# Cross attention on one core: probabilities transposed in 32x32 blocks on DVE, context in sixteen 32x32 tiles of TensorE

## What is computed

```python
q = x @ Wq + 2 * (x @ Aq @ Bq)        # x (8, 256, 1024), 32 heads of 32
k = c @ Wk + 2 * (c @ Ak @ Bk)        # c (8, 256, 1024), 8 key heads of 32
v = c @ Wv + 2 * (c @ Av @ Bv)        # each key head serves 4 query heads
attn = softmax(q @ k.T / sqrt(32))    # per head, 256 x 256
context = attn @ v
out = x + context @ Wo + 2 * (context @ Ao @ Bo)
```

## Time and profile before

| | before |
|---|---|
| median of 3 runs | 756.59 us (755.97 to 759.47) |
| span of the profiled execution | 753.1 us; the page gives no other time for it |
| PE, DVE, ACT, POOL busy | 98%, 62%, 51%, 46% |
| DMA | 117.01 MB, mean 155 GB/s |

### The profile page before, as it was taken

How to read it: one execution, slowest core, us unless ns; L and a number is a source line. 1 busy time by engine, 2 the same in 40 slices (tenths; PEclk the granted TensorE clock), 3 DMA queues, 4 the chain that set the end, 5 groups by cost and what they waited for, 6 DMA issues and landing times.

```text
span 753.1 us, 17856 instructions
## 1 busy us (share of the span) xinstructions
PE 737.6 (98%) x5776; PEld 645.2 (86%) x5776; DVE 469.0 (62%) x988; ACT 382.0 (51%) x1287; POOL 349.1 (46%) x322
## 2 busy tenths in 40 slices
PE   7899999999999999999999999999999999999998
PEld 6678899889989989999998998999867788888886
DVE  5957687687768668767876866787696412212211
ACT  4437665666666666666666666665685210111100
POOL 4757645745654574565557457555766100000000
PEclk9999999999999999999999999999999999999999
DMA  7775544554453555345454544645464834343331
GB/s 257 271 219 164 169 140 140 159 172 122 139 174 126 157 152 163 119 139 175 138 156 149 155 131 128 172 139 178 139 181 154 276 130 156 117 167 111 111 111 56
DMA packets 94665, 117.01 MB, mean 155 GB/s; under 512 B 8624, under 2 KB 76208, under 8 KB 94640
## 3 DMA queue, kind: packets, MB, share of 16 engines
q1 hardware_dynamic: 94640, 116.69, 49.3%
HBM read 78.91 MB, written 37.75 MB: 155 GB/s over the span
## 4 chain that ended last, share of the span: by engine, by line
PE 88%; DVE 5%; DMA 2%; issue 2%; POOL 1%; ACT 0%; SPq 0%; POOLq 0%; DVEq 0%
PE banks L868 32%; PE banks L917 23%; PE banks L897 15%; PE banks L906 8%; PE banks L882 7%; DVE neg_max L718 2%; PE banks L853 2%; DVE x_lo L725 2%; DMA probs_t<-wq 1%; PE banks L855 1%; DMA probs<-b4q 1%; DMA probs_t<-b4kv 1%; POOL k_stack L510 1%; DVE lora L679 0%; DVE probs_t L263 0%
## 5 line engine op out<-in xcount | busy, mean ns | idle before, releaser
L525 POOL TENSOR_TENSOR probs<-probs,rsums 128x512 f32<-128x512 f32 x256 | 266.4, 1041 | 205.4 <-DVE rsums L750 204.6
L582 ACT ACTIVATE probs<-banks,neg_max 128x256 f32<-128x256 f32 x512 | 238.7, 475 | 175.7 <-DVE neg_max L718 170.8
L718 DVE TENSOR_REDUCE neg_max<-banks 128x2 f32<-128x512 f32 x256 | 174.3, 682 | 20.0 <-PE banks L882 20.0
L897 PE MATMUL banks<-ident,probs 128*128 128x128 f32 x1024 | 157.1, 276 | 2.2 <-POOL probs L525 2.0
L263 DVE COPY probs_t<-banks 128x512 f32<-128x512 f32 x192 | 132.4, 690 | 43.0 <-PE banks L897 35.6
L868 PE MATMUL banks<-x_hi,w_hi 128*128 128x256 f32 x512 | 145.7, 285 | 0.8 <-POOL w_lo L500 0.4
L868 PE MATMUL banks<-x_hi,w_lo 128*128 128x256 f32 x512 | 144.6, 282 | 0.0
L868 PE MATMUL banks<-x_lo,w_hi 128*128 128x256 f32 x512 | 144.5, 282 | 0.0
L897 PEld LDWEIGHTS banks<-ident,probs 128*128 128x128 f32 x1024 | 115.5, 140 | 30.8 <-issue 27.1
L882 PE MATMUL banks<-k_stack,q_stack 96*128 96x256 f32 x512 | 122.8, 322 | 0.0
L582 ACT ACTIVATION_READ_ACCUMULATOR probs<-banks,neg_max 128x1 f32 x512 | 104.0, 203 | 0.0
(11 more groups left out here) (76 smaller groups left out, 1112.9 us busy)
## 6 DMA issues: line engine op xcount, KB each, us to landing
q_stack<-q_parts SPq DMA_DIRECT2D x192, 128.0 KB, 2.5
q_parts<-q_stage SPq DMA_DIRECT2D x64, 256.0 KB, 2.2
raw<-ct SPq DMA_DIRECT2D x32, 256.0 KB, 3.9
raw<-xt SPq DMA_DIRECT2D x32, 256.0 KB, 4.4
context<-ctx_stage SPq DMA_DIRECT2D x64, 128.0 KB, 1.8
probs<-xn SPq DMA_DIRECT2D x16, 512.0 KB, 4.1
out<-raw SPq DMA_DIRECT2D x15, 512.0 KB, 2.9
probs_t<-context SPq DMA_DIRECT2D x7, 1024.0 KB, 5.9
```

What stands on the lines that cost most here:

```text
L525: nc.gpsimd.tensor_tensor(probs[:, c], probs[:, c], rsums[:, c, :].unsqueeze(2).broadcast_to([P, 2, S]), ALU.mult).then_inc(norm_done, 1)
L582: last = nc.scalar.activation(probs[:, c, h, :], score_bank[c][:, S * h:S * (h + 1)], ACT.Exp, bias=neg_max[:, c, h:h + 1], scale=-1.0, ac ...
L718: nc.vector.tensor_reduce(out=neg_max[:, c, :], in_=score_bank[c].rearrange("p (h t) -> p h t", h=2), axis=AXIS, op=ALU.min).then_inc(max_ ...
L897: last = nc.tensor.transpose(bank[:, P * (2 * t + h):P * (2 * t + h + 1)], probs[:, c, h, P * t:P * (t + 1)], ident[:])
```

## The change

The probabilities are no longer transposed by PE. After normalisation, DVE transposes each slot's 128x512 tile in 32x32 blocks with one instruction, from `probs` to `turned_p`. A block lies then on the quarter of the partitions that its queries had: keys of one block of 32 on partitions, its queries along the row. So the context is computed by 32x32 tiles of PE: tile row `r` takes query block `r`, tile column `h` the head, and eight key blocks are accumulated. Each matmul has 32 rows, 32 columns and 64 moving columns (two query halves of 32). Four PSUM banks hold the results, one for each tile row. V must lie on all four quarters: it is sent to DRAM (`send_v`) and read back four times (`load_v`) into `v_rep`.

Two score banks are left instead of four: `AHEAD` becomes 2 and `NORM_AHEAD` 1. The turn copies on DVE and ACT go, and the context copy moves from DVE to ACT. The order of projection groups changes (V earlier in the body, q 3 instead of v 1 last in the prologue), SP's order follows, and the output products that were in slots 28 to 31 of the last batch come after the slots, around the last context. The waits at the head of a PE slot are now for the exponentials of that slot alone; DVE's transpose waits for the normalisation and, once a unit, for an older context. A constant of the DMA setup gets smaller to make room.

```diff
-AHEAD = 4
-NORM_AHEAD = 3
+AHEAD = 2
+NORM_AHEAD = 1
...
-            ("q", 3, 0), ("v", 1, 0)]
-PRO_Q = 3
+            ("q", 2, 0), ("q", 3, 0)]
+PRO_Q = 4
...
-        ("q", 0, 1), ("q", 1, 1), ("q", 2, 1), ("q", 3, 1), ("v", 0, 1), ("v", 1, 1)]
+        ("q", 0, 1), ("q", 1, 1), ("v", 0, 1), ("v", 1, 1), ("q", 2, 1), ("q", 3, 1)]
...
+KB = S // 32
...
-        v_sb = sb("v_sb", [P, 2, KV], F32)
+        v_stage = sb("v_stage", [P, 2, KV], F32)
+        v_rep = sb("v_rep", [P, KB, KV], F32)
...
-        probs_t = sb("probs_t", [P, 2, 2, GH, S], F32)
+        turned_p = sb("turned_p", [P, 2, 4, 2, KB, 32], F32)
...
-        score_bank = [banks[:, i, :] for i in range(4)]
-        turn_bank = [banks[:, 4 + i, :] for i in range(2)]
+        score_bank = [banks[:, i, :] for i in range(2)]
+        ctx_bank = [banks[:, 2 + i, :] for i in range(4)]
...
+            def load_v(m, fills, contexts):
+                cols = slice(P * m, P * (m + 1))
+                wait(v_stored, fills * DMA)
+                if contexts is not None:
+                    wait(ctx_mm, ctx_count(contexts))
+                for r in range(4):
+                    sp.dma_start(v_rep[32 * r:32 * (r + 1), :, cols],
+                                 v_dram[:, cols].rearrange("(k p) n -> p k n", p=32)).then_inc(v_in[m], DMA)
...
+                if c == 1 and not prologue:
+                    u = unit - 1
+                    act.wait_ge(ctx_mm, b * NG + ctx_count(u + 1))
+                    act.wait_ge(ctx_stored[u % 2], b * (4 * DMA) + DMA * (u // 2 + 1))
+                    nc.scalar.activation(
+                        ctx_stage[:, u % 2, :].rearrange("p (a r q) -> p r a q", a=2, r=4),
+                        banks[:, 2:6, 0:64].rearrange("p r (a q) -> p r a q", a=2),
+                        ACT.Copy).then_inc(ctx_done, 1)
...
+                if not (last and s >= SLOTS):
+                    dve.wait_ge(norm_done, n + (s + 1))
+                    if c == 0 and not prologue:
+                        dve.wait_ge(ctx_mm, b * NG + ctx_count(unit - 1))
+                    nc.vector.transpose(turned_p[:, unit % 2, c].rearrange("p h k q -> p (h k q)"),
+                                        probs[:, c].rearrange("p h t -> p (h t)")).then_inc(turned, 1)
...
-            def context(unit):
+            def context(b, u):
+
+                pe.wait_ge(turned, b * SLOTS + (4 * u + 4))
+                pe.wait_ge(ctx_done, b * NG + evicted(u))
...
+                for k in range(KB):
                     for h in range(GH):
-                        last = nc.tensor.matmul(
-                            bank[HD * h:HD * (h + 1), 0:S],
-                            v_sb[:, t, HD * (unit % NG):HD * (unit % NG + 1)],
-                            probs_t[:, unit % 2, t, h, :], start=(t == 0), stop=(t == 1),
-                            tile_position=(0, HD * h))
+                        for r in range(4):
+                            rows = slice(32 * r, 32 * (r + 1))
+                            moving = turned_p[rows, u % 2].rearrange("p (a g) h k q -> p k g h a q", a=2)
+                            last = nc.tensor.matmul(
+                                ctx_bank[r][HD * h:HD * (h + 1), 0:64],
+                                v_rep[rows, k, HD * u:HD * (u + 1)], moving[:, k, h // 2, h % 2],
+                                start=(k == 0), stop=(k == KB - 1), tile_position=(32 * r, HD * h))
...
-                    turn(unit, c)
...
+                    pe.wait_ge(exp_done, n + (s + 1))
+                    scores(n + (s + AHEAD), nxt % NG, turn)
...
+            pe.wait_ge(exp_done, NB * SLOTS)
+            for k in range(GROUP_MM):
+                out_step(0, 0, 0, k)
+            context(NB - 1, NG - 1)
+            for k in range(GROUP_MM):
+                out_step(0, 1, 0, k)
...
-    nc = bacc.Bacc("TRN2", target_bir_lowering=False, num_devices=1)
+    nc = bacc.Bacc("TRN2", target_bir_lowering=False, num_devices=1,
+                   dynamic_dma_scratch_size=1024)
```

More of the change, by code:

```diff
@@ L145, in xattn @@
         k_stacked = [sem(f"k_stacked{i}") for i in range(2)]
+        v_stored = sem("v_stored")
+        v_in = [sem(f"v_in{i}") for i in range(2)]
         ctx_stored = [sem(f"ctx_stored{i}") for i in range(2)]
@@ L239, in fold_bank @@
         def fold_bank(f):
[L240 removed]
+            return banks[:, f % 4, :] if f < FOLD_O else proj_bank[f % 2]
         def w_piece(f, part):
@@ L352, in _ @@
                 stack_k(m, 1, None)
-            for g in range(4):
+            send_v(PRO_Q)
+            for g in range(2):
                 send_q(g, g + PRO_Q + 1)
-                if g < 2:
-                    stack_q(g, 1, None)
+                stack_q(g, 1, None)
+            for m in range(2):
+                load_v(m, 1, None)
+            send_q(2, PRO_Q + 3)
             stack_q(2, 2, 4)
@@ L452, in _ @@
                 load_rows(0, h)
-            wait(ctx_mm, NB * NG)
+            wait(ctx_mm, ctx_count(NB * NG))
             load_ctx(2, 0)
@@ L608, in _ @@
                     high(c_hl, 2 + f, c_hi_done, 1)
-            for g in range(4):
+            for g in range(3):
                 if g == 2:
@@ L613, in _ @@
             stack_ready(act, 2)
-            for m in range(4):
+            act.sem_inc(ctx_done, evicted(0))
+            for m in range(AHEAD):
                 exps(m, m)
@@ L742, in _ @@
                 if f == FOLD_Q:
-                    proj_low("v", 0, 0, PRO_Q - 1, None, None)
-            for g in range(4):
+                    for i in range(2):
+                        proj_low("v", i, i, 2 + i, None, None)
+            for g in range(3):
                 if g == 2:
@@ L943, in _ @@
                     pe.wait_ge(proj_out, j - 1)
-                for k in range(GROUP_MM if j < PRO - 1 else V1_EARLY):
+                for k in range(GROUP_MM if j < PRO - 1 else Q3_EARLY):
                     inputs_ready(kind, i, k, 0)
@@ L954, in slot @@
                 unit, c = s // 4, s % 4
[L955 to L963 removed]
                 if not (last and s + AHEAD >= SLOTS):
[L965 to L966 removed]
+                    nxt, turn = divmod(s + AHEAD, 4)
+                    if turn == 0:
                         if nxt < NG:
```

174 lines of the change are left out of this document (70 added, 104 removed).

## The result

The changed kernel takes 1098.27 us in the median of four runs (1086.43 to 1108.23) against 756.28 (755.08 to 759.47) for the kernel before on the same chip: a ratio of 1.44 (95% interval 1.4323 to 1.4477). I had forecast 745 in a range of 690 to 828, so the prediction was wrong, and its range was wrong too. The profiled execution spans 1106.4 us, where that of before spans 753.1. The four executions of the changed kernel differ with their clock (1108.23 us at a mean granted clock of 0.857, 1086.43 at 0.884), and the ratio is taken from the faster ones.

What follows compares the result with a forecast made beforehand. PE, busy 98%, was taken to bound the kernel. A unit of 5.24 + 2.1 + 0.2 + 0.2 = 7.74 us against 8.21 gave −26.3 over 56 units; jumps +7, last batch +8, and 3.5 over the span: 745 us, range 690 to 828.

Steps and rivals of the forecast that it cites:

- the 2.1: Context on PE: forecast duration in us, chosen between 0.9 and 3.5 with a code-fetch floor of 1.9.
- one packet at a time: Context code: each packet starts only when the one before is entered; context 2.9 us, kernel 799 us; chance 0.22.
- issue of small pairs: Context on PE: pairs issue 0.032 us apart, 8.2 us a context, kernel 1087 us; chance 0.09.
- a context of over 6 us: Sign in the profile after: a context group lasting over 6 us means that issue of small matmuls binds.
- The engine's part: Context streaming on PE: 0.9 us if all sixteen tiles overlap, 3.5 if only the four column tiles do.
- break-even: Context duration at which the change neither gains nor loses: 2.3 us.
- Jumps back, +7: PE's loop over batches: seven rounds each jump to code that is gone, one packet of 1.0 us each, +7 us.
- Two score banks: 0.2 us: Scores wait for exponentials two slots back; it fits, with 0.2 us a unit of waiting charged in place of 0.14.
- DMA: nothing charged: V's store and reads on SP: covered, nothing urgent queued behind, no cost; without cover some 2 us a batch.
- the rival of the score chain: DVE's transpose before row maxima makes scores bind: 1.48 us a slot, unit 8.4, kernel 782 us; chance 0.08.
- The last batch, +8: Output products follow the slots instead of filling slots 28 to 31, and DVE sets the late slots: +8 us.
- 985: Kernel time in us if matmuls start never less than about 25 ns apart, making a context 6.4 us.

Runs made afterwards that it cites:

- e1: Changed kernel with each unit's 128 context calls issued by a loop of 8 turns over 16 calls, key blocks 1 to 7 left out: 941.82 us, ratio 1.2401.
- e12: Changed kernel with 4 of the 8 key blocks in the context, written straight: 838.83 us, ratio 1.112.
- e3: Kernel before, complete, with PE's loop over seven batches written out as straight code: 756.14 us, ratio 0.9997.
- e11: Changed kernel with context calls issued by a loop of 4 turns over 32 calls, key blocks 2 to 7 left out: 936.97 us, ratio 1.2371.
- e7: Changed kernel with 32 moving columns in place of 64 in every context matmul, second query half left out: 1086.53 us, ratio 1.4416.
- e6: Changed kernel, complete, with each context cut into pieces of 3, 3 and 2 key blocks over three slots: 971.21 us, ratio 1.2835.
- e4: Changed kernel, complete, with PE's loop over seven batches written out as straight code: 1048.64 us, ratio 1.3868.
- e2: Changed kernel with only the first of 8 key blocks in the context: 759.13 us, ratio 1.0072.
- e5: Changed kernel with one key block in the context and V sent and read back only in the prologue: 735.28 us, ratio 0.9709.
- e9: Changed kernel with one key block, V moved only in the prologue, q stack 2 loaded behind the next batch's inputs: 730.72 us, ratio 0.9652.

## Why the prediction was wrong, step by step

**What held.** A slot fell to 11 x 0.119 = 1.31 us as said (two scores start at 401.82 and 403.14 in the changed kernel, 1.32 apart). DVE's transpose takes 0.692 us (forecast: 0.69), and DVE, ACT and POOL stayed covered: their busy time is 44, 34 and 32% of the span. The tiles do run side by side in both directions: 128 matmuls with their loads start within about 1.3 us, where four at a time, at the prediction's 0.055 us each, would need 1.76. The new loop doesn't stay in the engine (168 packets; some 150 forecast), PE's idle time is put down to issue inside contexts, and the slower side had this mechanism as its rival.

**The step that failed** is "if the new loop is fetched anew in each round, a context can't pass faster than 2 x 0.96 = 1.9 us", with the 2.1 taken from it. It priced a packet by its transfer. The transfer did take about that (1.14 us), but what PE lives by is the distance from one packet's first instruction to the next one's: 3.71 us in the mean of 17, of which 1.18 lie ahead of the transfer and 1.39 behind it, with a gap of 2.46 us in the mean of 71. The rival "one packet at a time" had the right form, trigger and landing beside the transfer, but took its wait from a small DMA's 1.7 us and only one to two of them: 2.9 us for a context, 799 for the kernel. A context took 6.0 in the mean and 7.6 in the timeline above. e1 shows the size of the step: the same number of small matmuls without the packets takes 4.2. e12 and e3 show its condition: one packet's worth of small matmuls a unit, or a loop of large ones, is hardly held up.

**The rival that came nearest in time, issue of small pairs at 1087 us, was wrong in cause.** It had 0.032 us for each pair, read from weight loads that waited for streams; measured are 0.010. I had also written that a context of over 6 us would mean issue of this kind. The contexts took 6.0 in the mean and up to 8.4, so their duration alone would have been misread. The gaps tell the two apart: dense pieces, a whole one 128 pairs long, and cuts at the same places in nearly every batch, not 256 evenly spaced pairs, and e1 takes the gaps away with the pairs left in.

**The engine's part** was placed between 0.9 and 3.5. A matmul of the context starts 0.0101 us after the last while nothing holds it up, so 256 take 2.6. The bounds held, but 2.6 is above the break-even of 2.3: by the prediction's own sum the changed kernel would have been slower than before even with its code at hand, by (2.6 − 2.3) x 56 = 17 us before any other loss. That version wasn't built, since the loops of e1 and e11 bring turns of their own, so this stays worked out. e7 shows that the size of the term is not in the columns, from which I had made its ends.

**A term that was missing** is the clock. In the kernel before PE never stands in the loop and the granted clock is 1.00; I kept that for the kernel after without a word. Now PE stands over and over, and the clock falls to the 1.2 GHz level: each of the 53 falls in the 56 units comes in or soon after a distance of over 1 us between two starts. Not every such gap has a fall, though: there are 86. Each stretch makes the projections behind it 0.21 in place of 0.12. Worked out from the starts it is some 86 of the 297 us in these units. It couldn't be taken out alone, so the split between gaps and clock is read from the trace, not shown by a run. The profiled executions agree with the order of the two: where gaps are fewer, the clock is higher (e6 0.949, e4 0.888, after 0.857). But e1 has a mean of 0.896 without the long gaps, with 7 of its 25 falls after a context of over 3 us in which PE stood no longer than a loop's turn, and e2 has 0.919 with its waits for transfers. So dense stretches of 32x32 tiles are at times followed by a fall as well, and why then is open.

**Jumps back, +7.** Seven rounds have six jumps back, not seven. At them PE stands 0.6 to 2.6 us in the changed kernel, 7.0 in all, and five of the six waits are put down to exponentials; so the term had about the right size. Where a jump stands alone it costs 3.4 to 3.9 us (e6). The longest gaps of the changed kernel are not at the jump. They lie in the third context of every batch, of the last one too, which is straight code: 3.7 to 6.0 us between two starts. There the packet's transfer starts only 1.3 to 3.5 us after PE has stopped, and the DMA engines are busy meanwhile, with a share of 0.68 to 0.99 in all eight places. Here is the one at 423.5 us in windows, with the input loads that SP had queued before it:

```profile
420.19 2.08 SPq L280 DMA_DIRECT2D raw<-xt  x4
```
```profile
420.00:423.50 3.50, 3.50 (x206) 3.32 (x204) 2.24 (x6) 2.04 (x8) 2.08 (x2) 1.00 0.81 207
423.50:425.90 2.40, 0.15 (x16) 0.00 (x0) 0.00 (x0) 0.00 (x0) 0.00 (x0) 1.00 0.92 314
```

That the packet waits there for these loads is read from the two falling together; no run takes them apart. The 40 us that straight code gave back in e4 are then not the jumps' alone: 31 of them are shorter issue waits at L934, mostly from fewer contexts cut twice. I can't divide the rest further.

**"Two score banks: 0.2 us" and "DMA: nothing charged".** In the changed kernel both are hidden by the slow context. e2 uncovers them: with its small context and the two switches a unit should take 5.24 + 0.33 + 0.2 + 0.2 = 6.0 and takes 8.01, which is 113 us over 56 units. V's transfers are 24 of them (e5), 3.4 a batch against the 2 that I had named for the case without cover; 89 us of the 449 are at the lower clock; most of the rest is PE standing before scores (24 gaps of 2.6 us), for query stacks or for exponentials. My step said that nothing behind them on SP was urgent. The input loads of the next batch were, and I hadn't looked for them; e9 moves that wait from ACT to PE, and what it removes, 5 us, is within the intervals. Scores waiting for exponentials, the rival of the score chain, show up in e2 as 41 us of late weight loads, but there exponentials are themselves late from inputs, so no run has that rival by itself.

**The last batch, +8.** What follows the start of the last context grew by 6 us; the rest of that batch lies among the units, and I didn't separate it.

**The two pages.** The Trainium skill, Runtime: NRT & Kernel Launch, Instruction fetch mechanics, says that crossing a block of code is mostly hidden; e3 agrees with it (29 more packets, ratio 0.9997), and the changed kernel doesn't: 82 waits for issue at L934, 184.6 us. What decides is how long the instructions of a packet keep the engine. The Trainium skill, TensorE: Matmul & The Clock Gate, "Wait — 56ns, not 53.3ns?", would have matmuls start no less than about 25 ns apart; measured are 10, in bursts of 32 about 7.5. Its Part 3 with 4 ns lies on the other side of these. Both results of its own that I had given for these rules, 985 and a context of 1.0 us, are off, and that 985 is nearer to 1098 than my forecast is luck, since it reached that from another cause.

**What stays open.** What the 1.18 us ahead of a packet's transfer and the 1.39 behind it consist of, even where DMA is idle; what holds small matmuls at 0.010 us; and how the 86 us of the clock would move if the gaps were gone. No complete kernel that I ran beats the kernel before: the best was e6 at 971. Only e5 and e9 are under 756, and they leave out seven eighths of the context. Contexts whose two records a call are halved by another number format weren't tried.

## What to carry to other kernels

Before an operation is cut into small tiles, count the instructions of the loop body, before and after, and the time that each packet's worth of them (here 256 instructions) keeps the engine: 128 large matmuls with their loads last 15 us and hide the next packet, 128 small ones last 1.3 us and wait some 2.4 for it. Look then for the first thing that such waits break, which was TensorE's clock: a matmul that had nothing to do with the change took 0.21 us in place of 0.12 behind them. And price a supply that comes in pieces by the distance between two pieces, not by the length of one; where no row shows that distance, say so and let the range reach as far as a trigger, a transfer and a landing in a row would.

## What the runs showed of the hardware that was not expected

- A packet's code runs 1.19 to 1.61 us after its transfer of about 1.1 us has ended, at all gaps inside 56 contexts, and while PE works through a whole packet of small matmuls, the next transfer starts 1.18 us (mean of 17) after that packet's first matmul.
- Code of 616 matmul pairs (e1) stayed in the engine over the loop's rounds: 14 packets in the whole execution. 872 pairs (e11) did not: 72 packets.
- A 32x32 float32 matmul with its weight load starts each 0.010 us (64 columns) or 0.0086 (32 columns), 16 tiles side by side; at the lower granted clock 0.013. It isn't twice as long at half the clock, and hardly shorter with half the columns.
- A turn of a hardware loop on PE showed 0.26 us in which no weight load ran (e1, 477 such waits, 117.7 us), of which e11 makes it likely that a part was needed anyway.
- Straight code without a jump, with large matmuls in it, costs nothing: 0.9997 (0.9983 to 1.0011) with three times the packets.
- Four V reads hold SP for 1.80 us, 0.45 each, so that eight of them delay what is queued behind by 3.6 us in each batch.
